# Node stage of a graph layer: each tile's 128 by 128 product as four 64 by 64 products on the quarters of TensorE's array

## The chip, the cores and the metric

The kernel runs on one core of one Trainium2 chip. The metric is the device time of one execution in microseconds (us). Before the change three runs gave 929.51, 932.54 and 934.15 us, median 932.54.

## What is computed

A graph layer on 50,000 nodes of 160 numbers and 50,000 edges, everything in 32-bit floats. The edge stage makes one message of 160 numbers for each edge. The node stage averages the messages that arrive at each node, scales them with a gate `alpha`, adds them to `x + sc(x)`, and normalises each row. The change touches only `sc`:

```python
sc = jnp.concatenate([x0 @ Wsc0 * a * inv8,
      (jnp.einsum('num,uv->nvm', x1, Wsc1) * a[..., None] * inv32).reshape(n, 3 * MUL1)], axis=1)
...
x = _layernorm(x + sc + alpha * conv)
```

`x0` is the first 64 channels of a row, `x1` the other 96, which are three vectors of 32 channels; `a` is one number per node. In the kernel's order of channels the weight of `sc` is block-diagonal: a 64 by 64 block for `x0` and three 32 by 32 blocks for `x1`.

## The kernel before

The first 555 us or so are the edge stage: 392 tiles of 128 edges, four tiles in a step, messages written to DRAM in order of their destination. The node stage follows: 98 groups of 512 nodes (four tiles of 128), one group after the other. Each engine runs its own program, written out by hand; semaphores are all that ties them together. The programs of the node stage go by steps; in step s

- **TensorE** transposes the scaled inputs `xa` of group s into PSUM (L781, five 128 by 128 transposes, in the text T), then sums the messages of group s-1 by products of a one-hot matrix `hot` with the window of messages `win` (L795, twelve products on 60 rows, two halves of the array in turn, in the text A), then makes `sc` of group s-1 (L805 four products and L807 one, in the text S). T waits for `xa_ready` from GpSimd, A for `hot_ready` from VectorE, S for `xt_out` from ScalarE and for `pre_ready` of the group before from VectorE, since S overwrites the two PSUM banks that VectorE read.
- **VectorE** begins with the counts of group s-2 (`cnt`, L1305, waits for A's `agg_done`), copies the labels of window s (L1310, waits for the window's DMA), makes `hot` for group s (L1318), then small factors, then `pre = sc + x` of group s-2 (L1345, two instructions, one for each PSUM bank; waits for `sc_ready`), then `shift` of group s-5 (L1352), `coef` and the statistics of group s-4.
- **ScalarE** copies T's result to `xt` (L890, L892), scales the sums (`agg`, L900), takes roots and normalises three tiles in four (`fin`, L878), and issues the loads of `x` and the stores of the result.
- **GpSimd** makes `xa` of group s (L624, L628), adds `res = agg + pre` of group s-3 (L640), and normalises the fourth tile of group s-5 (`fin`, L649, waits for VectorE's `shift`), in that order; the next step's `xa` stands behind that `fin` in its queue.
- **SyncE** loads the window of group s as soon as A of group s-4 is done.

`xt` holds, for each of the four tiles, 128 channels by 128 nodes (64 of `x0`, 64 of `x1`), and as a fifth block the last 32 channels of all four tiles. L805 multiplies each of the first four blocks by a 128 by 128 weight `wy` of which two quarters are zero; L807 multiplies the fifth block by a block-diagonal weight, and so makes the last 32 channels of all four tiles at once. The results stand in two banks of PSUM: `sca_ps` (bank 4, four tiles by 128 outputs) and `scb_ps` (bank 5, four tiles by 32).

A 32-bit product is one row in the program and two records in the trace, each with its own weight load; a transpose is one.

Of the kernel before, what the change touches and what calls it, by code (L numbers as in the profile page):

```python
# [22 lines left out]
P = 128  # L23
# [6 lines left out]
MUL0, MUL1 = 64, 32  # L30
VEC = 3 * MUL1
# [14 lines left out]
GROUP = 4  # L46
# [24 lines left out]
HALF = 64  # L71
# [15 lines left out]
W_YA = W_E1 + P  # L87
W_Y1 = W_YA + MUL1 + 1 + MUL0
W_SA = W_Y1 + VEC + 1 + MUL0
W_SB = W_SA + P  # L90
W_Y1B = W_SB + P
WC = W_Y1B + VEC + 1 + MUL0
LAST = D - P


def gnn_kernel(nc, turned, spread, x_g, src_t, dst_t, dst_rows, sh_t, ea_t, weights, out):
# [22 lines left out]
    with ExitStack() as ctx:  # L119
        def sb(name, shape, dt=F32):  # L120
            return ctx.enter_context(nc.sbuf_tensor(name, shape, dt))
# [4 lines left out]
        ps = ctx.enter_context(nc.psum_tensor("ps", [P, 8, 512], F32))  # L126
        wt = sb("wt", [P, WC])
        wy = sb("wy", [P, WC - W_YA])
# [64 lines left out]
        xt = sb("xt", [P, 2, GROUP + 1, P])  # L193
# [34 lines left out]

        xt_ps = ps[:, 0:2, :].rearrange("p c (k e) -> p (c k) e", e=P)
        agg_ps = [ps[:, n:n + 2, :].rearrange("p c (k e) -> p (c k) e", k=2) for n in (2, 6)]  # L230
        sca_ps = ps[:, 4, :].rearrange("p (k w) -> p k w", k=GROUP)
        scb_ps = ps[:, 5, 0:P].rearrange("p (k w) -> p k w", k=GROUP)

        srcs_in = sem("srcs_in")
        tables_in = sem("tables_in")
# [125 lines left out]
        def group_alive(i, b, behind):  # L361
            return not isinstance(i, int) or 0 <= RING * i + b - behind < NG

        def group_has(i, b, behind):
            return not isinstance(i, int) or RING * i + b - behind >= 0

        def groups(i, b, behind=0):

            return RING * i + (b - behind + 1)

        def side(h):
            return slice(h * HALF, h * HALF + WP)
# [284 lines left out]
        def _(pe):  # L657
# [82 lines left out]
            def step(d):  # L740
                if alive(d, 0):
                    first_layer(d)
                for k in range(2):
                    if alive(d, 0):
                        turn(d, k)
                    if alive(d, 3):
                        combine(d - 3, k)
                if alive(d, 1):
                    weigh(d - 1)

            def spread_heads():

                pe.wait_ge(heads_ready, 1)
                for n in range(2):
# [7 lines left out]
                                 stop=True).then_inc(wrong_summed, 1)  # L762

            edge_steps(step, {1: spread_heads})

            pe.wait_ge(prepared, 1)
            with pe.If(pe.value_load(general_i[0:1, 0:1], min_val=0, max_val=1) != 0):
                with pe.Fori(0, T) as t:
# [3 lines left out]
                                     stop=True).then_inc(g_summed, 1)  # L772

            def step(i, b):
                if group_alive(i, b, 0):

                    if group_has(i, b, 1):
                        pe.wait_ge(xt_out, groups(i, b, 1))
                    pe.wait_ge(xa_ready, groups(i, b))
                    for k in range(GROUP + 1):  # L780
                        last = nc.tensor.transpose(xt_ps[:, k, :], xa[:, b % 2, k, :], ident[:])  # L781
                    last.then_inc(xt_ready, 1)
                if group_alive(i, b, 1):
                    b1 = (b - 1) % 2

                    if RING * i + b == 1:
                        for t in range(2):
                            pe.wait_ge(msg_ready[t], NQ)
                    pe.wait_ge(hot_ready, groups(i, b, 1))
                    if group_has(i, b, 3):  # L790
                        pe.wait_ge(agg_ready, groups(i, b, 3))
                    for k in range(2):
                        for c in range(WC_ROWS):
                            for h in range(2):
                                last = nc.tensor.matmul(  # L795
                                    agg_ps[b1][:, 2 * h + k, 0:SW], hot[side(h), b1, k, c, :],
                                    win[side(h), (b - 1) % RING, k, c, 0:SW],
                                    start=c == 0, stop=c == WC_ROWS - 1)
                    last.then_inc(agg_done, 1)

                    pe.wait_ge(xt_out, groups(i, b, 1))
                    if group_has(i, b, 2):
                        pe.wait_ge(pre_ready, groups(i, b, 2))
                    for k in range(GROUP):
                        nc.tensor.matmul(sca_ps[:, k, :], xt[:, b1, k, :],  # L805
                                         wy[:, W_SA - W_YA:W_SB - W_YA], start=True, stop=True)
                    last = nc.tensor.matmul(scb_ps.rearrange("p k w -> p (k w)"),  # L807
                                            xt[:, b1, GROUP, :],
                                            wy[:, W_SB - W_YA:W_Y1B - W_YA], start=True, stop=True)
                    last.then_inc(sc_ready, 1)  # L810


            pe.wait_ge(h_out, 2 * NS)
            pe.wait_ge(t_out, 2 * NS)
            node_steps(pe, step)


# [115 lines left out]
        def _(dve):  # L933
# [276 lines left out]
            for q in range(1, AHEAD):  # L1210
                prepare(q)

            edge_steps(step, {d: partial(between, d) for d in range(FLAG + 7)})

            dve.wait_ge(prepared, 1)
# [74 lines left out]
            def step(i, b):  # L1290
# [8 lines left out]
                nodes = (RING * i + b - 2) % X_RING  # L1299
# [36 lines left out]
                if adding:  # L1336
                    dve.wait_ge(ra_ready, g)
                    nc.vector.tensor_tensor(agg_ps[b0][:, :, GRA], agg_ps[b0][:, :, GATE],
                                            ra[:, b0], ALU.mult).then_inc(gra_ready, 1)

                    dve.wait_ge(sc_ready, g)
                    if group_has(i, b, 4):
                        dve.wait_ge(res_ready, groups(i, b, 4))
                    for sc, n, w in ((sca_ps, 0, P), (scb_ps, P, LAST)):
                        last = nc.vector.tensor_tensor(  # L1345
                            pre[:, b0, :, n:n + w], sc, xin[:, nodes, :, 1 + n:1 + n + w],
                            ALU.add)
                    last.then_inc(pre_ready, 1)
# [18 lines left out]

            dve.wait_ge(pads_ready, 1)
            node_steps(dve, step)


# [105 lines left out]
```

## Time and profile before

| | |
|---|---|
| runs | 929.51, 932.54, 934.15 us, median 932.54 |
| profiled execution, span from the first to the last instruction | 930.5 us |
| what lies around the span, as far as the median shows it | 2.0 us |
| busy share of the span | TensorE 95%, VectorE 87%, GpSimd 77%, ScalarE 68% |
| granted TensorE clock, mean | 0.995 |
| node stage, about | 555 to 918 us |
| TensorE busy from 600 to 700 us | 99.95 us of 100 |
| the 16 DMA engines, busy share from 600 to 700 us | 0.96, at 306 GB/s |

The profile has no time of the profiled execution other than its span, so a sum against the span is carried over to the median with the 2.0 us between them. The shares of the whole span mix two stages with different limits; the change lies in the node stage alone, which is read from its own stretch below. Starts of matmul records are when a record was issued; their ends are modelled, so a block's length is read from the start of its first record to the start of the next block's first.

### The profile page before, as it was taken

The page shows a single profiled execution, that of the slowest core. Times are in us where ns is not written, and L with a number is a line of the kernel's source. Part 1 is how long each engine was busy: PE and PEld are TensorE (multiplying, and loading weights), DVE is VectorE, ACT ScalarE, POOL GpSimd, SP SyncE. Part 2 cuts the span into 40 slices and gives each one's busy share as a digit, 9 for nine tenths or more (in the row PEclk, how much of TensorE's full clock was granted, in tenths as well). Part 3 has the DMA queues.
Part 4 walks back from the last instruction along what each step waited for, and adds up shares of the span by engine and source line. Part 5 has one row for each costly group of instructions (what it writes and reads, how often), then busy time and mean ns, then how long its engine had stood idle before and what let it go on. Part 6 is the DMA issues. An engine that isn't in the chain of part 4 may idle for free.

```text
span 930.5 us, 27956 instructions
## 1 busy us (share of the span) xinstructions
PE 880.9 (95%) x8336; PEld 758.5 (82%) x8336; DVE 812.1 (87%) x2797; ACT 632.5 (68%) x1961; POOL 714.5 (77%) x804
## 2 busy tenths in 40 slices
PE   3899999999999999999999889999999999999995
PEld 2778887888877878888888779989999898899994
DVE  3789999999988999999999978888888888888887
ACT  1555555555654555565565547888988888988887
POOL 6777777777777776777777318989998888989894
PEclk9999999999999999999999999999999999999998
DMA  6465554455565555456544227999999999999993
GB/s 181 118 178 159 163 143 127 133 140 131 140 133 133 168 156 150 132 160 181 153 131 133 86 84 231 305 305 302 303 302 301 300 304 295 300 306 308 304 298 136
DMA packets 87522, 186.47 MB, mean 200 GB/s; under 512 B 17647, under 2 KB 48139, under 8 KB 87372
## 3 DMA queue, kind: packets, MB, share of 16 engines
q1 hardware_dynamic: 48411, 87.72, 29.1%
q10 hardware_dynamic: 20016, 61.15, 19.7%
q0 software_dynamic: 18944, 35.81, 17.8%
q8 instruction: 69, 1.13, 0.5%
q14 instruction: 82, 0.66, 0.2%
HBM read 119.66 MB, written 64.95 MB: 198 GB/s over the span
## 4 chain that ended last, share of the span: by engine, by line
PE 46%; POOL 22%; issue 17%; DVE 11%; DMA 3%; ACT 1%; POOLq 0%; DVEq 0%; ACTq 0%
PE ps L795 7%; POOL res L640 7%; PE ps L736 7%; POOL gat L587 6%; PE ps L715 5%; POOL xa L628 5%; PE ps L733 4%; PE ps L805 4%; PE ps L696 4%; PE ps L702 4%; DVE mid L977 3%; PE ps L678 3%; POOL xa L624 3%; DVE z L995 2%; DMA gat<-spread,srcs 2%
## 5 line engine op out<-in xcount | busy, mean ns | idle before, releaser
L587 POOL DMA_INDIRECT gat<-turned,srcs x196 | 190.8, 973 | 66.6 <-issue 61.8
L587 POOL DMA_INDIRECT gat<-spread,srcs x196 | 188.7, 963 | 61.8 <-issue 60.0
L855 ACT ACTIVATE e_sb<-ps 128x512 f32<-128x512 f32 x196 | 106.4, 595 | 123.1 <-PE ps L702 122.0
L795 PE MATMUL ps<-win,hot 60*128 60x162 f32 x2352 | 189.1, 306 | 0.7 <-DVE hot L1318 0.7
L736 PE MATMUL ps<-wy,mid 128*128 128x161 f32 x784 | 182.3, 314 | 0.0
L795 PEld LDWEIGHTS ps<-win,hot 60*128 60x128 f32 x2352 | 164.9, 186 | 17.1 <-issue 16.5
L1001 DVE SCALAR_TENSOR_TENSOR msg<-ps,sha,z 128x161 f32<-128x161 f32 x392 | 151.0, 385 | 14.0
L640 POOL TENSOR_TENSOR res<-agg,pre 128x640 f32<-128x640 f32 x98 | 152.2, 1553 | 9.9 <-ACT agg L900 9.9
L733 PE MATMUL ps<-wy,mid 128*128 128x97 f32 x784 | 141.6, 262 | 0.2 <-DVE mid L977 0.2
L977 DVE TENSOR_TENSOR mid<-ps,e_sb 128x512 f32<-128x512 f32 x196 | 133.2, 680 | 2.2 <-PE ps L715 2.2
L878 ACT ACTIVATE fin<-res,shift,rstd 128x160 f32<-128x160 f32 x292 | 132.2, 539 | 1.3 <-DVE shift L1267 1.3
L900 ACT ACTIVATE agg<-ps,coef 128x160 f32<-128x160 f32 x392 | 122.8, 409 | 6.3 <-DVE coef L1358 6.2
L733 PEld LDWEIGHTS ps<-wy,mid 128*128 128x128 f32 x784 | 123.5, 191 | 1.3 <-issue 0.7
L840 ACT ACTIVATE z<-ps 128x65 f32<-128x65 f32 x392 | 89.7, 229 | 46.0 <-PE ps L736 45.5
L736 PEld LDWEIGHTS ps<-wy,mid 128*128 128x128 f32 x784 | 119.2, 192 | 0.0
L805 PE MATMUL ps<-wy,xt 128*128 128x128 f32 x784 | 113.5, 288 | 0.4 <-DVE pre L1345 0.4
L805 PEld LDWEIGHTS ps<-wy,xt 128*128 128x128 f32 x784 | 94.9, 191 | 17.7 <-issue 17.5
L995 DVE TENSOR_TENSOR z<-ps,sha 128x96 f32<-128x96 f32 x392 | 97.9, 250 | 9.1 <-ACT z L840 2.5
L830 ACT ACTIVATE h_sb<-ps 128x128 f32<-128x128 f32 x196 | 54.4, 278 | 74.3 <-PE ps L678 64.7
L715 PE MATMUL ps<-h_sb,wt 64*128 64x256 f32 x784 | 102.0, 379 | 1.4 <-DVE mid L977 1.4
L628 POOL TENSOR_TENSOR xa<-xin 128x512 f32<-128x512 f32 x98 | 102.8, 1048 | 0.0
L832 ACT ACTIVATE t_sb<-ps 128x384 f32<-128x384 f32 x196 | 95.0, 485 | 0.0
(104 smaller groups left out, 1543.2 us busy)
## 6 DMA issues: line engine op xcount, KB each, us to landing
win<-rows SPq DMA_DIRECT2D x392, 114.6 KB
rows<-msg SPq DMA_DIRECT2D x98, 326.0 KB
out<-fin ACTq DMA_DIRECT2D x47, 640.0 KB, 5.4
xin<-x_g ACTq DMA_DIRECT2D x92, 322.0 KB, 4.4
gat<-turned,srcs POOLq DMA_INDIRECT x196
gat<-spread,srcs POOLq DMA_INDIRECT x196
eas<-ea_t SPq DMA_DIRECT2D x7, 384.0 KB, 4.8
xin<-x_g SPq DMA_DIRECT2D x6, 322.0 KB, 4.2
```

The costliest lines, as they stand in the source:

```text
L587: pool.indirect_dma_start(out=gat[:, slot, first:first + of.shape[1]], out_offset=None, in_=of, in_offset=bass.IndirectOffsetOnAxis(ap=src ...
L628: nc.gpsimd.tensor_tensor(xa[:, b0, 0:GROUP, :], xin[:, n, :, 1:1 + P], xin[:, n, :, 0:1].broadcast_to([P, GROUP, P]), ALU.mult).then_inc( ...
L640: nc.gpsimd.tensor_tensor(res[:, slot], agg[:, b3], pre[:, b3], ALU.add).then_inc(res_ready, 1)
L715: last = nc.tensor.matmul(w_ps[:, t, 2 * c * P:2 * (c + 1) * P], wt[half, w:w + P], h_sb[half, b].rearrange("p k e -> p (k e)"), start=Tru ...
L733: nc.tensor.matmul(y[:, t, 0:W_Y1 - W_YA], mid[:, q % 2, t, 0, k, :], wy[:, 0:W_Y1 - W_YA], start=True, stop=True)
L736: nc.tensor.matmul(y[:, t, W_Y1 - W_YA:YW], mid[:, q % 2, t, 1, k, :], wy[:, of:of + VEC + 1 + MUL0], start=True, stop=True).then_inc(y_re ...
L795: last = nc.tensor.matmul(agg_ps[b1][:, 2 * h + k, 0:SW], hot[side(h), b1, k, c, :], win[side(h), (b - 1) % RING, k, c, 0:SW], start=c == ...
L805: nc.tensor.matmul(sca_ps[:, k, :], xt[:, b1, k, :], wy[:, W_SA - W_YA:W_SB - W_YA], start=True, stop=True)
L878: last = nc.scalar.activation(fin[:, past, k, :], res[:, past, k, :], ACT.Identity, bias=shift[:, past, k:k + 1], scale=rstd[:, past, k:k ...
L900: last = nc.scalar.activation(agg[:, b0, k, :], agg_ps[b0][:, k, 1:1 + D], ACT.Copy, scale=coef[:, b0, k:k + 1])
L977: nc.vector.tensor_tensor(mid[:, q % 2, t].rearrange("p c k e -> p (c k e)"), w_ps[:, t], e_sb[:, t], ALU.mult).then_inc(mid_ready[t], 1)
L1001: nc.vector.scalar_tensor_tensor(out=msg[:, q % 2 * QUAD + n, 0:1 + D], in0=y[:, t, Y_A:Y_C], scalar=sha[:, ring, n, 0:1], in1=z[:, k, t, ...
```

## The change

S is written in another way. Each of the four products of L805 becomes four: 64 channels by 64 nodes as weights, 64 outputs as moving columns. The two zero quarters of `wy` are left out, and the 128 nodes of a tile are split in two halves, so that the four products of a tile lie on the four quarters of the array: row half h takes the channels (0: `x0`, 1: the first 64 of `x1`), column half n the nodes. Row half 0 writes to bank 4, row half 1 to bank 5, at the partitions of its 64 nodes. L807 stays one full product, but writes its outputs in bank 5 behind those of row half 1, as four runs of 32. So bank 4 now holds 64 outputs for each tile and bank 5 holds 96, and VectorE's two additions take 64 and 96 columns for each tile in place of 128 and 32.

```diff
-        sca_ps = ps[:, 4, :].rearrange("p (k w) -> p k w", k=GROUP)
-        scb_ps = ps[:, 5, 0:P].rearrange("p (k w) -> p k w", k=GROUP)
+        sca_ps = ps[:, 4, 0:GROUP * MUL0].rearrange("p (k w) -> p k w", k=GROUP)
+        scb_ps = ps[:, 5, 0:GROUP * VEC].rearrange("p (k w) -> p k w", k=GROUP)
...
                     for k in range(GROUP):
-                        nc.tensor.matmul(sca_ps[:, k, :], xt[:, b1, k, :],
-                                         wy[:, W_SA - W_YA:W_SB - W_YA], start=True, stop=True)
-                    last = nc.tensor.matmul(scb_ps.rearrange("p k w -> p (k w)"),
-                                            xt[:, b1, GROUP, :],
-                                            wy[:, W_SB - W_YA:W_Y1B - W_YA], start=True, stop=True)
+                        for sc, h in ((sca_ps, 0), (scb_ps, 1)):
+                            half = slice(h * HALF, (h + 1) * HALF)
+                            w = W_SA - W_YA + h * HALF
+                            for n in range(2):
+                                nodes = slice(n * HALF, (n + 1) * HALF)
+                                nc.tensor.matmul(sc[nodes, k, 0:HALF], xt[half, b1, k, nodes],
+                                                 wy[half, w:w + HALF], start=True, stop=True)
+                    last = nc.tensor.matmul(scb_ps[:, :, HALF:VEC], xt[:, b1, GROUP, :],
+                                            wy[:, W_SB - W_YA:W_Y1B - W_YA].rearrange(
+                                                "p (k w) -> p k w", k=GROUP),
+                                            start=True, stop=True)
                     last.then_inc(sc_ready, 1)
...
-                    for sc, n, w in ((sca_ps, 0, P), (scb_ps, P, LAST)):
+                    for sc, n, w in ((sca_ps, 0, MUL0), (scb_ps, MUL0, VEC)):
                         last = nc.vector.tensor_tensor(
                             pre[:, b0, :, n:n + w], sc, xin[:, nodes, :, 1 + n:1 + n + w],
                             ALU.add)
```

TensorE's program before, one step of the node stage, from T to the end of S; a row is a line, an operation with the tiles that it writes and reads, its output's size and a count, and the semaphores that it waits for:

```order
L781 MATMUL ps<-ident,xa 128x128 [waits xa_ready,xt_out]
L781 MATMUL ps<-ident,xa 128x128 x4
L795 MATMUL ps<-win,hot 128x162 [waits agg_ready,hot_ready]
L795 MATMUL ps<-win,hot 128x162 x11
L805 MATMUL ps<-wy,xt 128x128 [waits pre_ready,xt_out]
L805 MATMUL ps<-wy,xt 128x128 x3
L807 MATMUL ps<-wy,xt 128x128
```

After the change the same step reads (L811 is the new inner product, L813 the full one):

```order
L781 MATMUL ps<-ident,xa 128x128 [waits xa_ready,xt_out]
L781 MATMUL ps<-ident,xa 128x128 x4
L795 MATMUL ps<-win,hot 128x162 [waits agg_ready,hot_ready]
L795 MATMUL ps<-win,hot 128x162 x11
L811 MATMUL ps<-wy,xt 64x64 [waits pre_ready,xt_out]
L811 MATMUL ps<-wy,xt 64x64 x15
L813 MATMUL ps<-wy,xt 128x4x32
```

Sixteen products of 64 by 64 stand where four of 128 by 128 stood, so S has 34 records in place of 10; no wait is added or moved.

VectorE's program before, around the addition `pre`:

```order
L1338 TENSOR_TENSOR ps<-ps,ra 128x4 [waits ra_ready]
L1345 TENSOR_TENSOR pre<-ps,xin 128x4x128 [waits res_ready,sc_ready]
L1345 TENSOR_TENSOR pre<-ps,xin 128x4x32
L1352 SCALAR_TENSOR_TENSOR shift<-stats,ps 128x4 [waits rstd_ready,rstd_ps_ready]
L1358 TENSOR_TENSOR coef<-ps,ra 128x4 [waits gra_ready]
```

And after it, seven lines further down in the file:

```order
L1345 TENSOR_TENSOR ps<-ps,ra 128x4 [waits ra_ready]
L1352 TENSOR_TENSOR pre<-ps,xin 128x4x64 [waits res_ready,sc_ready]
L1352 TENSOR_TENSOR pre<-ps,xin 128x4x96
L1359 SCALAR_TENSOR_TENSOR shift<-stats,ps 128x4 [waits rstd_ready,rstd_ps_ready]
L1365 TENSOR_TENSOR coef<-ps,ra 128x4 [waits gra_ready]
```

The 640 columns are shared out differently between the two additions; the order stays.

## Rows read from the trace of the kernel before

**Rows 1.** Page, part 1: busy us (share of span) and instructions of each engine.

```profile
PE 880.9 (95%) x8336; PEld 758.5 (82%) x8336; DVE 812.1 (87%) x2797; ACT 632.5 (68%) x1961; POOL 714.5 (77%) x804
```

**Rows 2.** Busy time in a stretch of the node stage, columns named by its header.

```profile
core 0: us, PE busy (x) PEld busy (x) DVE busy (x) ACT busy (x) POOL busy (x), PEclk, DMA share, GB/s
600.00:700.00 100.00, 99.95 (x1050) 90.51 (x1049) 87.33 (x375) 89.26 (x269) 89.90 (x109) 1.00 0.96 306
```

**Rows 3.** Waits from 600 to 900 us: total us, times, longest.

```profile
DVE cnt L1305 <- PE ps L795: 34.9, 73, 0.7
POOL fin L649 <- DVE shift L1352: 31.4, 71, 1.9
ACT xt L890 <- PE ps L781: 25.9, 66, 0.4
...
DVE ps L1310 <- DMA win<-rows: 4.5, 7, 1.5
...
PE ps L781 <- POOL xa L628: 1.3, 2, 0.7
```

**Rows 4.** Timeline of TensorE, one step: start, us, line, operation, count.

```profile
660.93 1.93 PE L795 MATMUL ps<-win,hot 60*128 60x162 f32 x24
662.79 1.16 PE L805 MATMUL ps<-wy,xt 128*128 128x128 f32 x8
663.78 0.39 PE L807 MATMUL ps<-wy,xt 128*128 128x128 f32 x2
664.01 0.71 PE L781 MATMUL ps<-ident,xa 128*128 128x128 f32 x5
664.65 1.93 PE L795 MATMUL ps<-win,hot 60*128 60x162 f32 x24
```

**Rows 5.** Timeline in the edge stage: weight loads, then matmuls on halves.

```profile
303.50 0.24 PEld L696 LDWEIGHTS ps<-t_sb,wt 64*64 64x64 f32 x8 [0.26 <-ACT t_sb L832]
304.12 0.30 PEld L702 LDWEIGHTS ps<-t_sb,wt 64*128 64x128 f32 x4 [0.38 <-issue]
...
304.66 1.03 PE L715 MATMUL ps<-h_sb,wt 64*128 64x256 f32 x8
305.52 0.39 PE L670 MATMUL ps<-eas,wt 64*128 64x128 f32 x4
```

**Rows 6.** Groups by form, whole span: L696's quarter weight loads (busy us, mean ns, idle before).

```profile
L696 PEld LDWEIGHTS ps<-t_sb,wt 64*64 64x64 f32 x784 | 23.3, 132 | 37.9 <-ACT t_sb L832 29.3 <-issue 8.6
```

**Rows 7.** Timeline of VectorE and GpSimd in the step of rows 4.

```profile
662.91 0.16 DVE L1305 TENSOR_SCALAR cnt<-ps 128x4 f32<-128x4 f32 x1 [0.47 <-PE ps L795]
...
664.32 0.89 DVE L1345 TENSOR_TENSOR pre<-ps,xin 128x512 f32<-128x512 f32 x2
665.12 0.15 DVE L1352 SCALAR_TENSOR_TENSOR shift<-stats,ps 128x4 f32<-128x4 f32 x1
...
665.38 0.48 POOL L649 TENSOR_SCALAR fin<-res,rstd,shift 128x160 f32<-128x160 f32 x1 [0.35 <-DVE shift L1352]
...
666.18 1.05 POOL L628 TENSOR_TENSOR xa<-xin 128x512 f32<-128x512 f32 x1
667.18 1.56 POOL L640 TENSOR_TENSOR res<-agg,pre 128x640 f32<-128x640 f32 x1
```

**Rows 8.** Timeline of a step in which a window came late.

```profile
788.49 0.17 DVE L1310 COPY ps<-win 128x6 f32<-128x6 f32 x1 [1.05 <-DMA win<-rows]
...
791.69 1.05 POOL L628 TENSOR_TENSOR xa<-xin 128x512 f32<-128x512 f32 x1
...
792.89 0.74 PE L781 MATMUL ps<-ident,xa 128*128 128x128 f32 x5 [0.64 <-POOL xa L628]
793.55 1.93 PE L795 MATMUL ps<-win,hot 60*128 60x162 f32 x24
```

**Rows 9.** Groups by form, 600 to 900 us: the two additions `pre`, mean ns.

```profile
L1345 DVE TENSOR_TENSOR pre<-ps,xin 128x512 f32<-128x512 f32 x80 | 55.3, 691 | 0.0
...
L1345 DVE TENSOR_TENSOR pre<-ps,xin 128x128 f32<-128x128 f32 x80 | 22.4, 279 | 0.0
```

## The prediction

> **What bounds the kernel now.** The page's first part comes first: TensorE is busy for 95% of the span, VectorE 87%, GpSimd 77%, ScalarE 68% [rows 1]. These are means over two stages, and the change lies in the second, so the busy times of a stretch inside it come next: from 600 to 700 us TensorE is busy 99.95 us of 100, GpSimd 89.90, ScalarE 89.26, VectorE 87.33, the DMA engines 0.96 of the time, and the granted clock is 1.00 [rows 2]. TensorE is full there and the others are not far behind. The waits say who waits for whom: VectorE's `cnt` for A (34.9 us in 73 waits), GpSimd's `fin` for VectorE's `shift` (31.4 in 71), ScalarE's `xt` for T (25.9 in 66), while T waited for GpSimd's `xa` only twice, 1.3 us in all [rows 3]. So three engines idle 0.39 to 0.48 us at such a wait, each behind TensorE.
>
> TensorE's own step is A, S, T without a gap: from 660.93 A takes 1.86 us to the first record of S at 662.79, S takes 1.22 to T at 664.01, T 0.64 to the next A at 664.65 [rows 4]. The step is 3.72 us. The stage has 98 groups, so 97 such steps.
>
> **The change: S on TensorE.** Gone are the eight records of L805, to which 0.99 us belong, 662.79 to 663.78; the two of L807 stay and take 0.23 [rows 4], 0.115 each. Eight at 0.115 are 0.92, so 0.07 is the load that stands bare at the start of the block. In come 32 records on quarters. The edge stage has the nearest thing: L696, four products on the four quarters with 256 columns, eight records. From its first load at 303.50 to the next block's first load at 304.12 are 0.62 us [rows 5]. What one round of 256 columns costs is read from L715, eight records in pairs on halves, four rounds: 304.66 to 305.52, 0.86, so 0.215 a round [rows 5]. Two rounds are 0.43, so L696's eight records ran four abreast, and 0.19 of its 0.62 is the block's own: the first load, the stagger of the quarters, and the emptying of the array before the next block's shape.
>
> A round of 64 columns is a quarter of 0.215, 0.054, if it is the columns that count. The full record's 0.115 for 128 columns, where half of 0.215 is 0.108, shows 0.007 on top, so I take 0.061. The bounds are 0.054, and 0.115 if a round can't be shorter than a full record. Sixteen products of two records on four quarters are eight rounds: 0.49. S is then 0.19 + 0.49 + 0.07 (a bare load again ahead of the full product, which has a new shape) + 0.23 = 0.98 us, against 1.22: 0.24 saved in a step, with bounds of 0.30 saved and 0.19 lost. The full product now writes four runs of 32; no row shows such an output, so it may cost nothing (the rows' nearest, a run of 128 at 0.115) or twice, 0.23 more. I take nothing. TensorE alone would come to 3.48 us a step.
>
> The 0.19 holds a change of the array's shape that the kernel before had once less in a step. L702's loads stood 0.38 us behind L696's last, with no release to wait for [rows 5], and so does a shorter gap stand ahead of every A and S. The Trainium skill, "TensorEngine Tiling (Array Packing)", section Key Properties, says that a change of tiling mode drains the engine, which speaks against this change and agrees with those rows; if there were no such drain, the sum for S would be shorter by what of the 0.19 it holds.
>
> **VectorE, ScalarE, GpSimd.** `pre` takes 691 ns for 512 columns and 279 for 128 [rows 9]: 1.07 a column and 142 to begin with. With 256 and 384 columns it is 416 + 554 = 970, what it was. No wait is added. An earlier end of S brings VectorE nothing by itself: it begins `pre` at 664.32 [rows 7], when S, which ended where T began at 664.01 with records of 0.39 (663.78 + 0.39 = 664.17) [rows 4], is over.
>
> **What is late next.** The gain reaches the end only as far as T and A can begin earlier, and T waits for `xa`. Follow that: A from 660.93 lets VectorE begin `cnt` at 662.91; `shift` ends at 665.12 + 0.15 = 665.27; it releases GpSimd's `fin` at 665.38; the next `xa` stands behind that in GpSimd's queue and ends at 666.18 + 1.05 = 667.23 [rows 4, 7]. That is 6.30 us from A's start, none of it made shorter. What follows is seen where a window came late and T did wait: `xa` ended at 791.69 + 1.05 = 792.74, and the next A began at 793.55, 0.81 later [rows 8]. So from one A to the A two steps on are 6.30 + 0.81 = 7.11 us at the least, 3.555 a step. Before, two steps were 7.44, and the loop had 0.33 to spare. TensorE's 3.48 is below 3.555: the loop sets the step, and 0.165 of the 0.24 is kept. 97 x 0.165 = 16.0 us.
>
> **The DMA takes some back.** The engines are busy 0.96 of the time [rows 2], and seven windows of 80 came so late that VectorE waited, 4.5 us in all [rows 3]; once the loop has nothing to spare such a wait counts fully: at 788.49 VectorE waited 1.05, and with the 0.33 spare taken off that is near the 0.64 that TensorE then waited [rows 8]. With steps shorter by 4% the same bytes come in less time. Nothing before shows the share beyond 0.96 over 100 us; between no more waits (0) and all the gain (16), I charge about as much again as these waits are now, 5 us over the whole stage.
>
> Sum against the profiled execution: 930.5 - 16.0 + 5 = 919.5 us of span, and with the 2.0 that the median lies above it, 921.5.
>
> **Rivals.**
>
> *TensorE alone sets the step*, the loop having more to spare than I read: 3.48, so 97 x 0.24 = 23 us, 909 as a median. For it: no engine but TensorE has more than 90% of the stretch [rows 2]. Against: every term of the loop is a row.
>
> *The DMA is the wall.* 0.96 of 3.72 is 3.57 us of DMA work a step, close to the loop's 3.555; at a share of 0.98 the step is 3.64, which gives 97 x 0.08 = 8 us, and if 0.96 is all there is, nothing: 925 to 932.5, middle 929. For it: the share and the late windows. Against: windows are issued two steps ahead and only seven of 80 were waited for [rows 3].
>
> *The quarters run two abreast*, since two of them share a row half and its moving operand, and here sixteen follow one another where L696 had four: sixteen rounds of 0.061, 0.49 more, so S is 1.47 and the step 3.97. 97 x 0.25 = 24 us slower, 957. It decides from the point at which a round takes more than 0.061 + 0.24/8 = 0.091. For it: no row has quarters in more than two rounds, or with 64 columns. Against: L696's 0.62 us has no room for four rounds of 0.215 [rows 5].
>
> *The records can't be fed so fast.* S has 34 of them in place of 10. The densest long run is A, 24 in 1.86 us, 0.078 each [rows 4]; at that pace 34 take 2.6 us, 1.4 more a step, 97 x 1.4 = 138 us, 1070. Against: L696's eight loads were let go together by ScalarE's `t_sb`, and all had begun within 0.24 us less the 0.132 of the last, 0.11 [rows 5, 6], 0.014 for a load and its product. The Trainium skill, "TensorE: Matmul & The Clock Gate", section "Wait — 56ns, not 53.3ns?", names such a limit, about 62 ns for each matmul where the sequencer decodes in microcode; 34 of those are 2.1 us, an estimate by which the time would be about 1018. Those eight loads speak against it.
>
> **How the numbers follow.** Chances: my forecast 0.52, with its own range of 913 to 928; TensorE alone 0.08; the DMA as the wall 0.22; two abreast 0.13; feeding 0.05. The predicted time is the forecast's. The range leaves out the two slow rivals (0.18) and a little at the fast end: 908 to 938, which holds full gain, no gain, and rounds of up to about 0.095. About 0.5%, 4.7 us, is what a measurement of this kernel can tell from no change. Faster by more: the forecast and TensorE alone, and the quarter of the DMA case that keeps most of its 8 us, 0.64 in all; within it: the rest of the DMA case and the forecast's slow edge, 0.18; slower: the two slow rivals, 0.18.
>
> **What the profile after would show.** S from its first record to T in about 0.98 us, its quarter records in bunches of four; more than 1.22 means the rounds failed. T waiting for GpSimd's `xa` in most steps, not in two of 80; without that, TensorE alone or the DMA sets the step. GpSimd's wait for `shift` down from 0.44 to about 0.2 a step, and VectorE's for A likewise. VectorE's waits for windows at about twice 4.5 us; much more means the DMA is the wall. The two additions `pre` at about 416 and 554 ns. The granted clock still at 1.00: TensorE now waits about 0.1 us a step, which should not show there. My forecast is wrong if a round takes more than 0.09 us, if the loop is longer than its rows, or if the DMA engines can't go above 0.96.

## The result and the profile after

| | us, median (range) | ratio to the runs of before | 95% interval |
|---|---|---|---|
| before | 934.15 (929.51 to 936.31) | | |
| changed | 928.31 (926.40 to 931.75) | 0.9946 | 0.9921 to 0.9970 |

The change makes the kernel faster by 0.54%, 5.8 us by the medians. The forecast was 921.5, 11 us faster: the sign is right, the time lies inside the range, and the size is about half of what was forecast.

The profiled execution of the changed kernel has a span of 930.0 us, nearly that of before: it was the slowest of the nine (931.75 us), and the first A of its node stage came 2.3 us later. The node stage itself is read from the first and the last record of A (L795; kernel before, then changed):

```profile
L795 PE MATMUL ps<-win,hot x2352: 295/297/402, 552.8 to 917.5; 60*128 60x162 f32 x196
```

```profile
L795 PE MATMUL ps<-win,hot x2352: 294/298/634, 555.1 to 917.2; 60*128 60x162 f32 x196
```

The last record of a block of A starts 1.6 us after its first, so 97 steps took 917.5 - 552.8 - 1.6 = 363.1 us before, 3.74 each, and 360.5 after, 3.72 each. That is 2.6 us less, where the medians say 5.8; 1.4 us of the difference are the stage's first A, which took 558.44 - 555.14 = 3.30 us in place of 1.86, at a granted clock of 0.50, the lower of TensorE's two levels (1.2 GHz), after a wait of 0.68 for `hot`. The other eleven profiled executions wait as long there and show no such fall; why this one did is not known:

```profile
555.14 3.37 PE L795 MATMUL ps<-win,hot 60*128 60x162 f32 x24 [0.68 <-DVE hot L1325]
558.44 0.70 PE L811 MATMUL ps<-wy,xt 64*64 64x64 f32 x32
```

```profile
core 0: us, PE busy (x) PEld busy (x) DVE busy (x) ACT busy (x) POOL busy (x), PEclk, DMA share, GB/s
556.00:558.00 2.00, 2.00 (x19) 2.00 (x17) 0.07 (x1) 0.00 (x0) 0.02 (x1) 0.50 0.04 8
```

TensorE's step after, its timeline as in [rows 4]:

```profile
660.77 1.93 PE L795 MATMUL ps<-win,hot 60*128 60x162 f32 x24
662.63 0.69 PE L811 MATMUL ps<-wy,xt 64*64 64x64 f32 x32
663.25 0.49 PE L813 MATMUL ps<-wy,xt 128*128 128x128 f32 x2
663.58 0.71 PE L781 MATMUL ps<-ident,xa 128*128 128x128 f32 x5
664.22 1.93 PE L795 MATMUL ps<-win,hot 60*128 60x162 f32 x24
```

S takes 663.58 - 662.63 = 0.95 us in place of 1.22, and the step, where nothing is late, 3.45 in place of 3.72. That is the whole 0.27 that the quarters are worth, and 97 of them would be 26 us. So the question is where 20 of them went. The steps show it first. Blocks of A in the timeline of the changed kernel, one after the other:

```profile
574.67 1.93 PE L795 MATMUL ps<-win,hot 60*128 60x162 f32 x24
...
578.12 1.93 PE L795 MATMUL ps<-win,hot 60*128 60x162 f32 x24
...
581.78 1.93 PE L795 MATMUL ps<-win,hot 60*128 60x162 f32 x24
...
585.23 1.93 PE L795 MATMUL ps<-win,hot 60*128 60x162 f32 x24
```

The steps go 3.45, 3.66, 3.45: two of them are 7.11 us, which is what the prediction gave for the loop, its chain from an A over VectorE and GpSimd to the A two steps on. The loop's mean is 3.555, and the stage's mean is 3.72, so 0.16 more are lost in single long steps. The busy times and the waits from 600 to 900 us, as in [rows 2] and [rows 3]:

```profile
core 0: us, PE busy (x) PEld busy (x) DVE busy (x) ACT busy (x) POOL busy (x), PEclk, DMA share, GB/s
600.00:900.00 300.00, 287.20 (x5093) 247.13 (x5097) 262.95 (x1132) 272.10 (x812) 271.39 (x325) 1.00 0.96 306
```

```profile
DVE cnt L1312 <- PE ps L795: 25.6, 64, 0.7
POOL fin L649 <- DVE shift L1359: 24.9, 40, 1.6
...
PE ps L781 <- POOL xa L628: 10.9, 17, 0.9
DVE ps L1317 <- DMA win<-rows: 10.9, 13, 1.5
```

TensorE is no longer full (287.20 of 300 us; before, 298.23). It now waits for `xa`, 10.9 us in place of 1.3, and VectorE waits for windows 10.9 us in place of 4.5. The DMA share is 0.96, what it was. What one late window does, in VectorE's, GpSimd's and TensorE's timelines:

```profile
841.35 0.17 DVE L1317 COPY ps<-win 128x6 f32<-128x6 f32 x1 [1.21 <-DMA win<-rows]
```

```profile
843.75 0.48 POOL L649 TENSOR_SCALAR fin<-res,rstd,shift 128x160 f32<-128x160 f32 x1 [1.62 <-DVE shift L1359]
...
844.55 1.05 POOL L628 TENSOR_TENSOR xa<-xin 128x512 f32<-128x512 f32 x1
```

```profile
841.45 1.93 PE L795 MATMUL ps<-win,hot 60*128 60x162 f32 x24
843.73 0.69 PE L811 MATMUL ps<-wy,xt 64*64 64x64 f32 x32 [0.35 <-DVE pre L1352]
844.35 0.49 PE L813 MATMUL ps<-wy,xt 128*128 128x128 f32 x2
845.74 0.74 PE L781 MATMUL ps<-ident,xa 128*128 128x128 f32 x5 [0.90 <-POOL xa L628]
846.41 1.93 PE L795 MATMUL ps<-win,hot 60*128 60x162 f32 x24
```

VectorE waits 1.21 us for the window, `shift` is late, GpSimd's `fin` waits 1.62, the `xa` behind it is late, and T waits: this step is 846.41 - 841.45 = 4.96 us.

The late windows have a pattern. ScalarE issues a store of 640 KB every second step, and here one went out shortly before:

```profile
839.28 0.39 ACTq L922 DMA_DIRECT2D out<-fin  x1
```

Counted over the node stage, 14 windows made VectorE wait more than 0.2 us in the changed kernel and 8 in the kernel before; 13 of the 14, and all 8, belong to even groups, and VectorE's copies of them stand 0.9 to 2.4 us behind the issue of a store.

### The profile page after: what moved, and what is told of

Same layout as the page of the kernel before. It is cut to its first block, busy times and chain, and to the rows that moved or that the text cites. A ratio compares the mean times of both kernels' runs of the same rounds, so it can differ in the third digit from the quotient of the medians.

```text
span 930.0 us, 32660 instructions
## 1 busy us (share of the span) xinstructions
PE 867.5 (93%) x10688; PEld 731.0 (79%) x10688; DVE 811.5 (87%) x2797; ACT 635.4 (68%) x1961; POOL 714.2 (77%) x804
## 4 chain that ended last, share of the span: by engine, by line
PE 36%; POOL 26%; issue 19%; DVE 11%; DMA 5%; ACT 1%; POOLq 0%; ACTq 0%; DVEq 0%
POOL res L640 9%; POOL gat L587 7%; PE ps L736 7%; POOL xa L628 6%; PE ps L715 5%; PE ps L733 4%; PE ps L696 4%; PE ps L702 4%; DVE mid L984 3%; POOL xa L624 3%; PE ps L795 3%; PE ps L678 3%; DVE z L1002 2%; DMA out<-fin 2%; PE ps L676 2%
## 5 line engine op out<-in xcount | busy, mean ns | idle before, releaser
L795 PE MATMUL ps<-win,hot 60*128 60x162 f32 x2352 | 190.5, 308 | 0.7 <-DVE hot L1325 0.7
L795 PEld LDWEIGHTS ps<-win,hot 60*128 60x128 f32 x2352 | 166.4, 188 | 17.0 <-issue 14.4
L1002 DVE TENSOR_TENSOR z<-ps,sha 128x96 f32<-128x96 f32 x392 | 97.9, 250 | 10.9 <-ACT z L847 4.0
L1325 DVE TENSOR_TENSOR hot<-columns,ps 128x768 f32<-128x768 f32 x98 | 92.4, 943 | 0.1
L1352 DVE TENSOR_TENSOR pre<-ps,xin 128x256 f32<-128x256 f32 x196 | 87.1, 486 | 0.3 <-PE ps L813 0.2
```

The costliest lines, as they stand in the source:

```text
L795: last = nc.tensor.matmul(agg_ps[b1][:, 2 * h + k, 0:SW], hot[side(h), b1, k, c, :], win[side(h), (b - 1) % RING, k, c, 0:SW], start=c == ...
L1002: nc.vector.tensor_tensor(z[:, k, t, 1 + MUL0:].rearrange("p (m v) -> p m v", m=3), y[:, t, 0:MUL1].unsqueeze(1).broadcast_to([P, 3, MUL1] ...
```

## The experiments

Two theories after the result. D: the DMA engines' volume is the wall, that is the limit that sets the mean step, 0.96 being all they give. L: windows that are asked for late, in a loop that has nothing to spare. Ratios below are to runs of the kernel before on the same chip.

**Less to move.** In the store of results:

```diff
-                    act.dma_start(block_rows(out, n),
-                                  fin[:, 2 * (n % 2):2 * (n % 2) + 2].rearrange(
-                                      "p g k w -> p (g k w)")).then_inc(stored[n % 2], 16)
+                    act.dma_start(block_rows(out, n)[:, 0:2 * D],
+                                  fin[:, 2 * (n % 2), 0:2].rearrange(
+                                      "p k w -> p (k w)")).then_inc(stored[n % 2], 16)
```

> The changed kernel with each store of results (L922 of the changed file, 640 KB every second step) cut to its first quarter, 160 KB; the rest of the result is not stored. Bytes of two steps fall from 2204 to 1724 KB. Theory D (the DMA engines' volume is what took the gain back): the waits for windows on VectorE go from 10.9 us (600 to 900 us) to under 2, the steps settle at the loop's 3.555 us, and the time is 910 to 916 us. Rival R (the long steps have another cause than the DMA volume): the waits stay and the time is 925 to 930.

> The kernel before with the same cut of the stores. Theory D: TensorE's own 3.72 us sets the step, only the 4.5 us of waits for windows can go, so 928 to 933 us. If stores cost the kernel time in another way, both kernels with the cut fall by the same amount, and this one is at 920 or below.

Measured: changed kernel with the cut 918.44 us, ratio 0.9828 (0.9795 to 0.9861); kernel before with the cut 931.04, 0.9961 (0.9940 to 0.9981). The cut gives the changed kernel about 11 us and the kernel before 3.5. The waits of the changed kernel with the cut:

```profile
PE ps L781 <- POOL xa L628: 3.8, 7, 0.9
DVE ps L1317 <- DMA win<-rows: 2.8, 5, 1.4
```

The windows' waits fall from 10.9 to 2.8 us (D said under 2), and the time is some 2 us above the range that theory D gave and 6.6 below R's. So most of the long steps do come from the DMA's side; R is out. It doesn't tell volume from lateness, since fewer bytes also make a window land sooner.

**The loop opened.** GpSimd's program with `fin` of one group earlier moved behind `xa`:

```diff
                     nc.gpsimd.tensor_tensor(
                         xa[:, b0, 0:GROUP, :], xin[:, n, :, 1:1 + P],
                         xin[:, n, :, 0:1].broadcast_to([P, GROUP, P]), ALU.mult
                     ).then_inc(xa_ready, 1)
+                old = RING * i + b - 6
+                if 0 <= old < NG - LAST_GROUPS:
+                    ... (fin of group old, as it was)
                 if group_alive(i, b, 3):
                     ... (res)
-                old = RING * i + b - 5
-                if 0 <= old < NG - LAST_GROUPS:
-                    ... (fin of group old)
```

> The changed kernel with GpSimd's program in another order: xa of a group stands ahead of fin of an older group (one step older than now), so that xa no longer waits for VectorE's shift. This opens the loop of 7.11 us per two steps. Theory D: the DMA volume sets the mean step, which stays at about 3.71, so 924 to 930 us, with TensorE's waits for xa gone and its waits moved to hot, behind the windows. Rival L (the loop is what holds the mean step, because it has nothing to spare for a late window): the steps go to TensorE's own 3.45 with the late windows absorbed, 903 to 915 us.

> The kernel before, full products, with xa ahead of fin on GpSimd. Its TensorE sets the step at 3.72 us and its loop has 0.33 us to spare in two steps, so opening the loop alone should bring little, only the few steps that a late window made longer: 930 to 934 us. If it brings as much as on the changed kernel (about 6 us), the gain of the open loop has nothing to do with the quarters.

Measured: on the changed kernel 921.85 us, 0.9853 (0.9826 to 0.9880); on the kernel before 930.51, 0.9977 (0.9956 to 0.9997). On the changed kernel that is 6 to 9 us better than without, between what D and L gave; on the kernel before, 2 us. The two longest waits of the changed kernel with the loop open:

```profile
DVE ps L1317 <- DMA win<-rows: 32.0, 28, 3.1
ACT agg L907 <- DVE coef L1365: 26.3, 24, 2.1
```

T no longer waits for `xa`. VectorE now waits mostly for windows, 32.0 us of the 300 (4.9 for A), and such a wait holds back `pre` and with it S. One late window, 3.12 us of waiting at 600.5 us, made a step of 7.04 us, and TensorE's clock fell behind it, so that this execution lost more there than the window alone would cost:

```profile
core 0: us, PE busy (x) PEld busy (x) DVE busy (x) ACT busy (x) POOL busy (x), PEclk, DMA share, GB/s
603.00:609.00 6.00, 6.00 (x63) 5.51 (x63) 3.94 (x16) 5.52 (x18) 4.62 (x6) 0.50 0.71 207
```

**As little work on TensorE, without quarters.**

```diff
-                    for k in range(GROUP):
+                    for k in range(2):
                         nc.tensor.matmul(sca_ps[:, k, :], xt[:, b1, k, :],
```

> The kernel before with two of the four products of L805 left out, so that S has six full records and TensorE's own step is 3.72 - 4 x 0.115 = 3.26 us, without any quarters. Theory D with the loop of 3.555 us: as little gain as the quarters brought, 924 to 931 us. Rival Q (the quarters themselves cost something elsewhere, in PSUM or in their feeding): this one is clearly faster than the changed kernel, 905 to 918 us.

Measured: 928.26 us, 0.9932 (0.9907 to 0.9957). TensorE's own step fell by 0.45 in place of 0.27 (3.27 us in the stage's first four steps), and the time by the same 6 us. Its blocks of A, further on:

```profile
841.67 1.93 PE L795 MATMUL ps<-win,hot 60*128 60x162 f32 x24
...
845.00 1.93 PE L795 MATMUL ps<-win,hot 60*128 60x162 f32 x24
...
848.78 1.93 PE L795 MATMUL ps<-win,hot 60*128 60x162 f32 x24
```

Two steps are 7.11 us once more, with another S: the loop doesn't depend on TensorE's own step. Q is out: the quarters cost nothing elsewhere that shows, and the next thing to be late gives the time.

**Loop open and less to move.** Both edits above in one kernel:

> The changed kernel with xa ahead of fin on GpSimd and with the stores cut to a quarter: the loop is open and the DMA has 22% less to move; the rest of the result is not stored. If loop and DMA volume are the two things that took the gain, TensorE's own 3.45 us sets the step: 97 x 0.27 us below the kernel before, 905 to 910 us. Rival: a third bound stands close behind (ScalarE or GpSimd, both above 0.92 busy with the cut alone), and the step stays at 3.52 or more, 912 to 917 us.

Measured: 906.38 us, 0.9714 (0.9687 to 0.9742). The rest of the gain is back. No third bound stands in the way yet, though GpSimd is busy for 96.7 us of 100 and is now the nearest:

```profile
600.00:700.00 100.00, 99.38 (x1821) 87.42 (x1819) 93.43 (x404) 95.04 (x289) 96.72 (x115) 1.00 0.89 258
```

**Windows asked for sooner, the same bytes.** The ring of window buffers goes from four to six; the places that index it follow:

```diff
-        win = sb("win", [P, RING, 2, WC_ROWS, AW])
+        win = sb("win", [P, W_RING, 2, WC_ROWS, AW])
...
-                if group_has(i, b, RING):
-                    sp.wait_ge(agg_done, groups(i, b, RING))
+                if g >= W_RING:
+                    sp.wait_ge(agg_done, g - W_RING + 1)
```

> The changed kernel with six window buffers in place of four, so that a window is asked for two steps sooner. The bytes are the same; the loop is closed as in the changed kernel. If the DMA engines could do more than 0.96 and only the late asking for windows keeps them from it (theory A), late windows go away and the step falls to the DMA's 1100 KB at 313 GB/s, 3.60 us, or the loop's 3.555: 916 to 922 us. If 0.96 is all that they do with this mix of packets (theory V), nothing changes: 925 to 930 us.

> The changed kernel with six window buffers and with xa ahead of fin on GpSimd. With the loop open and windows asked for sooner only the DMA's volume is left: 3.60 us a step at the highest rate seen, 313 GB/s, so 97 x 0.15 us below the kernel before, 915 to 920 us. If the six buffers bring something beyond the open loop, it is faster than the open loop alone (921.85); if not, equal to it.

> The kernel before, full products, with six window buffers and with xa ahead of fin on GpSimd: all that the fastest version has but the quarters. If TensorE's 3.72 us sets the step as soon as nothing is late, 928 to 932 us, and the quarters' own worth with nothing behind them to be late is the distance to 906.96: 97 x (3.72 - 3.45) = 26 us less what late windows cost here. Rival: buffers and order alone bring most of the gain, and this version comes below 920.

Measured: six buffers with the loop closed 922.06 us, 0.9880 (0.9851 to 0.9908); six buffers with the loop open 906.96, 0.9721 (0.9699 to 0.9742); the same two edits on the full products 930.12, 0.9960 (0.9944 to 0.9975). With the loop closed no wait for a window is left among the waits, but two others are (L650 and L782 are `fin` and T of this file):

```profile
POOL fin L650 <- DVE shift L1361: 11.8, 36, 0.5
POOL fin L650 <- DMA out<-fin: 8.9, 9, 1.6
...
PE ps L782 <- POOL xa L629: 6.2, 8, 1.2
```

The loop of 3.555 us a step is 10 us above 3.45, so 917; the waits of `fin` for a store, 8.9 us, which stand in the same loop, fit the rest up to 922: of the nine steps longer than 3.9 us in this trace, eight hold such a wait, and the other is the one in which GpSimd's first `fin` falls. With both edits, TensorE and the busy times are:

```profile
661.41 1.93 PE L796 MATMUL ps<-win,hot 60*128 60x162 f32 x24
663.27 0.69 PE L812 MATMUL ps<-wy,xt 64*64 64x64 f32 x32
663.89 0.49 PE L814 MATMUL ps<-wy,xt 128*128 128x128 f32 x2
664.22 0.71 PE L782 MATMUL ps<-ident,xa 128*128 128x128 f32 x5
664.86 1.93 PE L796 MATMUL ps<-win,hot 60*128 60x162 f32 x24
```

```profile
600.00:700.00 100.00, 100.00 (x1833) 88.09 (x1831) 94.24 (x407) 96.30 (x292) 97.43 (x117) 1.00 1.02 328
700.00:800.00 100.00, 99.87 (x1827) 87.80 (x1825) 94.13 (x407) 95.25 (x291) 96.75 (x117) 1.00 1.01 331
```

TensorE is full again, at 3.45 us a step. The DMA engines move 328 and 331 GB/s, against 306 in the changed kernel and in the kernel before, with the share at 1.02 and 1.01: theory D as a wall is out and L is what is left, and the expectation of 915 to 920, which took 313 GB/s for the highest rate, was too careful. The whole output is computed and stored here; at 0.9721 this version is faster than both kernels. Against the same two edits on the full products, 930.12, the quarters are worth 23 us.

| | as it was | loop open | six buffers | both |
|---|---|---|---|---|
| full products | 934.15 | 930.51 | not run | 930.12 |
| quarters | 928.31 | 921.85 | 922.06 | 906.96 |

**The order of the quarters.** In the fastest version the four tiles go inside the loops over the quarters, so that eight records in a row fall on one quarter:

```diff
-                    for k in range(GROUP):
-                        for sc, h in ((sca_ps, 0), (scb_ps, 1)):
+                    for sc, h in ((sca_ps, 0), (scb_ps, 1)):
...
-                            for n in range(2):
+                        for n in range(2):
+                            for k in range(GROUP):
```

> The fastest version with the sixteen quarter products in another order: all four tiles on one quarter, then all four on the next, so that eight records in a row go to the same quarter; the results are the same. If TensorE looks far enough ahead to start the other quarters anyway, S stays at 0.95 us and the time at 907. If records of one quarter hold up those behind them, up to 32 rounds of about 0.06 follow one another in place of eight: S up to 2.4 us, the step up to 4.9 and the time up to 1050; the place in between says how far it looks ahead.

Measured: 989.63 us, 1.0581 (1.0547 to 1.0614). S in its timeline:

```profile
662.14 1.54 PE L812 MATMUL ps<-wy,xt 64*64 64x64 f32 x32
663.61 0.49 PE L814 MATMUL ps<-wy,xt 128*128 128x128 f32 x2
663.94 0.71 PE L782 MATMUL ps<-ident,xa 128*128 128x128 f32 x5
```

The 32 quarter records take 663.61 - 662.14 = 1.47 us in place of 0.62, S 1.80 in place of 0.95, and 97 x 0.85 = 82 us is the whole loss. This lies between the two cases of the expectation. The starts of the 32 records in this block fall into four rows of eight, 0.058 us from one to the next but for 0.107 behind the first, and each row begins beside the fifth record of the row before. Read as one row for each quarter, which the trace doesn't name, TensorE starts a record on another quarter ahead of three that still wait, and not further ahead. The order of the change, one product on each quarter in turn, is what gives four abreast.

## Why the prediction was right or wrong

**S, right.** Forecast 0.98 us, measured 0.95. The 32 quarter records and the emptying behind them took 0.62 (forecast 0.68), the full product 0.33 (0.30); its four runs of 32 cost little that shows. TensorE's own step is 3.45 (3.48).

**VectorE's additions, right.** Forecast 416 + 554 ns; in the changed kernel, 600 to 900 us:

```profile
L1352 DVE TENSOR_TENSOR pre<-ps,xin 128x384 f32<-128x384 f32 x81 | 44.4, 548 | 0.0
...
L1352 DVE TENSOR_TENSOR pre<-ps,xin 128x256 f32<-128x256 f32 x81 | 34.4, 424 | 0.0
```

**The loop, right.** Forecast 7.11 us for two steps; measured 3.45 + 3.66 = 7.11, and 7.11 again with another S. The sign that T would wait for `xa` in most steps came out in part: from 600 to 900 us T began later than 0.33 us behind S's full product in 42 of 80 steps, in 24 of them by some 0.18, and the view of the waits lists only the 17 longer ones. GpSimd's wait for `shift` came to 24.9 us, about 0.31 a step, where 0.2 was forecast. The granted clock was 1.00 from 600 us on, as forecast; the stage's first A, at the lower level, was not foreseen.

**The charge for late windows, wrong in size.** This is the term that failed: 5 us of the 16 were to be lost, and by the medians 16.0 - 5.8 = 10.2 were. In the profiled executions the stage's mean is 3.72 in place of the loop's 3.555, so 97 x 0.16 = 16 us stand above the loop, 1.4 of them the first A; before, 97 x 0.02 = 2 stood above TensorE's 3.72, and the sum had left room for those 2 and its 5. Two things are in it. The waits for windows grew from 4.5 to 10.9 us in 300, where the profile after was to show about twice 4.5; that is near. But the sum charged only the growth, and took the waits of before as paid for, although the prediction itself says that once the loop has nothing to spare such a wait counts fully. The waits of before had been paid for by the 0.33 us that the loop had to spare: with that used up by the shorter step, the old ones count too. Over the whole span they are 13.1 us in 16 waits, close to the 14 us that stand above the loop without the first A:

```profile
DVE ps L1317 <- DMA win<-rows: 13.1, 16, 1.5
```

The late window at 841.35 shows the same in one step: 1.21 us of waiting made a step of 4.96, 1.4 longer than the loop's 3.555.

**The rivals.** The DMA as the wall had the right number, 929, by luck, and the wrong mechanism: with the same bytes the engines went to 331 GB/s once windows were asked for two steps sooner and `xa` stood ahead of `fin`. TensorE alone setting the step (909) is what the kernel does when those two are done, 906.96. Two abreast and slow feeding are out for this order: 32 records in 0.62 us are 0.019 each.

**Open.** Which transfers a late window stood behind, with the engines 0.96 busy, is not settled. That nearly all late windows follow the issue of a store, and that most of the waiting goes when the stores are cut, speaks for the stores; a store moved to another step was not tried. The runs show that fewer bytes or an earlier request make the lateness harmless. The first profile's 0.33 us of spare and the share of 0.96 both pointed at it, and neither gave its size.

## What to carry to other kernels

When the engine that sets the pace is made faster, count the slack of every loop behind it, and charge every wait that this slack has absorbed so far, not only the new ones: the same saving of 0.27 us a step was worth 6 us here, and 23 us once one instruction had moved in another engine's queue and a ring had two more buffers. A DMA share of 0.96 did not say that the engines can give no more; a version with earlier requests and the same bytes tells that in one run. Products on quarters are best tried going round the quarters, one product each, as neighbours in the program: the other order cost 82 us here.

## What the runs showed of the hardware that was not expected

- TensorE's look-ahead across quarters is short: 32 records that go round the quarters take 0.62 us, the same records with eight in a row on one quarter 1.47.
- One wait can cost clock as well: with the loop open, TensorE waited 2.26 us for a late window's `pre`, and from 603 to 609 us the granted clock was 0.50, the lower of its two levels (1.2 GHz), so that A took 3.55 us in place of 1.86.
- A DMA share of 0.96 at 306 GB/s was not full: 331 GB/s in another version with the same transfers, at a share of 1.01.
- Late windows and the closed loop hide each other's cost: either edit alone brings 6 to 9 us, both together 21.
